# A 16-key band on attention weights: an added mask in TensorE's accumulation, or a product on VectorE behind the sigmoid

## The reference, cut to what matters

```python
idx = t - 1 - w                       # w = 0..15
valid = idx >= 0
nb = where(valid, z[:, clip(idx)], 0) # keys and values of the window
tau = sigmoid(einsum('bthd,bthwd->bthw', q, nb_k) / sqrt(8))
msg = einsum('bthw,bthwd->bthd', tau, nb_v)
y = x + msg.reshape(B, T, D) @ wo.T   # then a layer norm over D, gamma, beta
```

## Time and profile before

| | |
|---|---|
| median of 3 runs | 229.62 us (228.37 to 230.73) |
| the profiled execution | 228.22 us |
| its span in the trace | 226.5 us |
| span by the granted TensorE clock, mean | 0.856 |
| second attention, first scores to last value matmuls | 81.41 to about 128 us of the span |

### The profile page before, as it was taken

How to read it: one execution, slowest core, us unless ns; L and a number is a source line. 1 busy time by engine, 2 the same in 40 slices (tenths; PEclk the granted TensorE clock), 3 DMA queues, 4 the chain that set the end, 5 groups by cost and what they waited for, 6 DMA issues and landing times.

```text
span 226.5 us, 4763 instructions
## 1 busy us (share of the span) xinstructions
PE 176.7 (78%) x1677; PEld 132.3 (58%) x1677; DVE 115.2 (51%) x353; ACT 115.0 (51%) x268; POOL 63.3 (28%) x93
## 2 busy tenths in 40 slices
PE   2769689999997969995999959999720009999990
PEld 1327467776654534653568537999620008999980
DVE  6466685479855420530161479796475003555530
ACT  3756633886778555861463816422490003556540
POOL 8998002005200040000020020000674720355442
PEclk9979955799999788996799988999955555999996
DMA  4456355290003510250000399000000338000000
GB/s 118 123 129 191 73 177 153 53 335 6 9 1 85 174 35 0 87 170 26 3 0 3 103 367 269 4 3 0 3 0 23 117 114 283 26 16 26 26 10 0
DMA packets 21085, 18.91 MB, mean 84 GB/s; under 512 B 4029, under 2 KB 18608, under 8 KB 21062
## 3 DMA queue, kind: packets, MB, share of 16 engines
q1 hardware_dynamic: 19606, 16.86, 24.9%
q0 software_dynamic: 896, 1.59, 2.1%
q10 hardware_dynamic: 560, 0.16, 0.3%
HBM read 8.54 MB, written 4.03 MB: 55 GB/s over the span
## 4 chain that ended last, share of the span: by engine, by line
PE 59%; DVE 12%; DMA 8%; SPq 7%; issue 5%; POOL 4%; ACT 4%; DVEq 0%; POOLq 0%
PE ps L1018 7%; SPq L394 6%; PE ps L1031 6%; PE ps L891 6%; PE ps L611 5%; PE ps L848 5%; DMA t_Ks<-t_parts 4%; PE ps L828 4%; PE ps L677 4%; PE ps L814 3%; PE ps L606 3%; POOL z_dram L589 3%; DVE t_mx L1413 3%; PE ps L817 3%; PE ps L714 2%
## 5 line engine op out<-in xcount | busy, mean ns | idle before, releaser
L1325 ACT ACTIVATE t_v_pad<-ps,t_b_tile 128x128 f32<-128x128 f32 x60 | 17.2, 368 | 32.2 <-PE ps L1018 32.2
L1168 ACT ACTIVATE t_P<-ps 128x512 f32<-128x512 f32 x32 | 19.1, 603 | 18.4 <-PE ps L817 18.2
L1413 DVE TENSOR_REDUCE t_mx<-ps 128x4 f32<-128x512 f32 x32 | 21.8, 688 | 10.8 <-PE ps L677 10.3
L1136 ACT ACTIVATE t_P<-ps 128x512 f32<-128x512 f32 x32 | 18.8, 601 | 8.3 <-PE ps L700 3.9
L559 POOL TENSOR_SCALAR t_rstd<-t_mv 128x4 f32<-128x4 f32 (+2 forms) x5 | 1.4, 279 | 75.0 <-DVE t_mv L1482 75.0
L594 POOL DMA_INDIRECT out_dram<-t_v_pad,t_Qs x15 | 15.1, 1006 | 25.1 <-DVE t_v_pad L1684 24.4
L1018 PE MATMUL ps<-t_zsT,t_late 128*128 128x128 f32 x120 | 17.8, 297 | 0.2 <-DVE t_zsT L1680 0.2
L1010 PE MATMUL ps<-t_ident,t_Qs 128*128 128x128 f32 x15 | 4.3, 304 | 16.9 <-DMA t_Qs<-z_dram 16.9
L814 PE MATMUL ps<-t_bandb,t_identb 128*128 128x512 bf16 x32 | 13.5, 421 | 4.9 <-DMA t_Ks<-t_parts 4.9
L1542 DVE SCALAR_TENSOR_TENSOR t_Qs<-t_v_pad,t_mod,t_blend 128x128 f32<-128x128 f32 x64 | 17.1, 347 | 0.1
L1031 PE MATMUL ps<-t_Ks,t_v_pad 128*128 x120 | 16.9, 284 | 0.0
(11 more groups left out here) (265 smaller groups left out, 361.9 us busy)
## 6 DMA issues: line engine op xcount, KB each, us to landing
t_Qs<-t_parts SPq DMA_DIRECT2D x24, 128.0 KB
t_Ks<-t_parts SPq DMA_DIRECT2D x24, 128.0 KB
t_Ks<-in_L_ffn_W_dram SPq DMA_DIRECT2D x1, 2048.0 KB, 9.5
z_dram<-t_empty_row SPq DMA_DIRECT2D x1, 1935.0 KB, 8.5
t_Qs<-z_dram SPq DMA_DIRECT2D x1, 1032.0 KB, 6.9
t_Qs<-z_dram SPq DMA_DIRECT2D x1, 645.0 KB, 4.2
t_rows<-in_fside_BxSxS_dram SPq DMA_DIRECT2D x2, 256.0 KB, 3.2
t_x_tok<-in_x_dram SPq DMA_DIRECT2D x2, 256.0 KB, 3.7
```

The lines of the kernel that those rows point to most:

```text
L1136: act.activation(P[:, u % 3, :], SCORE_BANKS[u % 2][:, :], ACT.Exp, scale=SCALE).then_inc(scores_read, 1)
L1168: act.activation(P[:, (UNITS + u) % 3, :], ps[u % 4][:, :], ACT.Sigmoid, scale=SCALE).then_inc(window_scores_read, 1)
L1325: m = act.activation(hsT[:, n % 2, cs], ps[n % 2][:, cs], ACT.Gelu, bias=b1_tile[:, n % 2, c:c + 1])
L1413: dve.tensor_reduce(mx[:, b, 4 * g:4 * g + 4], MAX_BANKS[u % 2][:, :].rearrange("p (j t) -> p j t", j=4), AX.X, ALU.max).then_inc(max_scor ...
```

## The change

The band is no longer added to the scores. PE's matmul with `bandb` is gone, and each of the four score matmuls starts its own part of the bank. ACT takes the sigmoid of all 128x128 pairs. Then DVE multiplies the four heads' weights in place by `band`, a 32-bit matrix of ones and zeros (`keep_band`, one instruction of 128x512 a unit, placed last but for the residual in the unit's turn). PE's value matmuls wait for DVE's product in place of ACT's sigmoid. Since a unit's weights are alive for longer, `P` has four buffers instead of three, and the value matmuls and the output of a batch come one turn later (`LAG_WVALUES` 3, `LAG_WOUT` 6). `FRONT_AT` is computed from `LAG_WOUT` and moves by a turn too. The first attention uses the four buffers as well.

```diff
@@ -48,7 +48,7 @@
 
         ident = sb("ident", [128, 128])
         identb = sb("identb", [128, 128], BF16)
-        bandb = sb("bandb", [128, 128], BF16)
+        band = sb("band", [128, 128])
         onesb = sb("onesb", [128, 128], BF16)
         ones_row = sb("ones_row", [1, NT], BF16)
         mask_rows = sb("mask_rows", [NB, T], BF16)
@@ -90,7 +90,8 @@
         negmT = sb("negmT", [H, NB, T], BF16)
         sshift = sb("sshift", [128, NB, H])
         w_self = sb("w_self", [128, NB, H])
-        P = sb("P", [128, 3, 512])
+        RING = 4
+        P = sb("P", [128, RING, 512])
         pv_sb = sb("pv_sb", [128, 2, 256])
         den = sb("den", [128, 2, H])
         rden = sb("rden", [128, 2, H])
@@ -218,7 +219,7 @@
         HANDOFF = [half * HALF * G + HALF * G - 1 + LAG_OUT for half in range(2)]
 
         WINDOW_AT = UNITS + LAG_VALUES
-        LAG_WVALUES, LAG_WOUT = 2, 5
+        LAG_WVALUES, LAG_WOUT = 3, 6
         TURNS = WINDOW_AT + UNITS + LAG_WOUT
 
         FRONT_AT = WINDOW_AT + HALF * G - 1 + LAG_WOUT + 6
@@ -503,11 +505,11 @@
             pool.iota(empty_row[:, TOKEN:TOKEN + 1].bitcast(I32), pattern=[[0, 1]], base=NT, channel_multiplier=1)\
                 .then_inc(tile_zero, 1)
 
-            link(pool.memset(bandb[:], 0.0))
-            link(pool.affine_select(bandb[:], bandb[:], pattern=[[1, 128]], compare_op=ALU.is_ge,
-                                    fill=MASKED, base=-1, channel_multiplier=-1))
-            pool.affine_select(bandb[:], bandb[:], pattern=[[-1, 128]], compare_op=ALU.is_ge,
-                               fill=MASKED, base=WINDOW, channel_multiplier=1).then_inc(band_ready, 1)
+            link(pool.memset(band[:], 1.0))
+            link(pool.affine_select(band[:], band[:], pattern=[[1, 128]], compare_op=ALU.is_ge,
+                                    fill=0.0, base=-1, channel_multiplier=-1))
+            pool.affine_select(band[:], band[:], pattern=[[-1, 128]], compare_op=ALU.is_ge,
+                               fill=0.0, base=WINDOW, channel_multiplier=1).then_inc(band_ready, 1)
             pool.wait_ge(ld_braw, 16)
             pool.tensor_copy(b_parts[:, 0, :], b_raw[:]).then_inc(b_split, 1)
             pool.wait_ge(b_split, 1)
@@ -712,7 +714,7 @@
                         pe.wait_ge(pv_read, b - 1)
                 for j in range(4):
                     m = pe.matmul(VALUE_BANKS[b % 2][32 * j:32 * j + 32, g // 2 * T:(g // 2 + 1) * T],
-                                  v_pad[:, b, pair_head(g, j), :], P[:, u % 3, j * T:(j + 1) * T],
+                                  v_pad[:, b, pair_head(g, j), :], P[:, u % RING, j * T:(j + 1) * T],
                                   start=(g % 2 == 0), stop=(g % 2 == 1))
                 m.then_inc(pv_done, 1)
 
@@ -805,28 +807,26 @@
                 if u == 0:
                     pe.wait_ge(max_scores_read, G * NB)
                     pe.wait_ge(scores_read, G * NB)
-                    pe.wait_ge(band_ready, 1)
                 if b % HALF == 0 and g == 0:
                     pe.wait_ge(stack_in[half_of(b)], 16 * (4 * NSLOT + 2))
                 if u >= 4:
                     pe.wait_ge(window_scores_read, u - 3)
                 bank = ps[u % 4]
-                pe.matmul(bank[:, :], identb[:], bc_mid(bandb[:], 4), start=True, stop=False)
                 for j in range(4):
                     h = quad_head(g, j)
-                    m = pe.matmul(bank[:, j * T:(j + 1) * T], stacked(Ks, b, h), stacked(Qs, b, h), start=False,
-                                  stop=(j == 3))
+                    m = pe.matmul(bank[:, j * T:(j + 1) * T], stacked(Ks, b, h), stacked(Qs, b, h), start=True,
+                                  stop=True)
                 m.then_inc(window_scores_full, 1)
 
             def window_values(b, g):
                 u = b * G + g
-                pe.wait_ge(window_scores_read, u + 1)
+                pe.wait_ge(banded, u + 1)
                 if g == 0:
                     job_wait_read(pe, f"bv_{half_of(b)}")
                     pe.wait_ge(pv_read, NB + b - 1)
                 for j in range(4):
                     m = pe.matmul(VALUE_BANKS[b % 2][32 * j:32 * j + 32, 0:T], v_pad[:, b, quad_head(g, j), :],
-                                  P[:, (UNITS + u) % 3, j * T:(j + 1) * T], start=(g == 0), stop=(g == G - 1))
+                                  P[:, (UNITS + u) % RING, j * T:(j + 1) * T], start=(g == 0), stop=(g == G - 1))
                 m.then_inc(pv_done, 1)
 
             def window_out(b):
@@ -1131,9 +1131,9 @@
                 if u == 0:
                     job_wait_read(act, "ks_0")
                     job_wait_read(act, "ks_1")
-                if u >= 3:
-                    act.wait_ge(pv_done, u - 2)
-                act.activation(P[:, u % 3, :], SCORE_BANKS[u % 2][:, :], ACT.Exp, scale=SCALE).then_inc(scores_read, 1)
+                if u >= RING:
+                    act.wait_ge(pv_done, u - RING + 1)
+                act.activation(P[:, u % RING, :], SCORE_BANKS[u % 2][:, :], ACT.Exp, scale=SCALE).then_inc(scores_read, 1)
 
             def shift_row(b):
 
@@ -1164,8 +1164,8 @@
 
             def window_weights(u):
                 act.wait_ge(window_scores_full, u + 1)
-                act.wait_ge(pv_done, UNITS + u - 2)
-                act.activation(P[:, (UNITS + u) % 3, :], ps[u % 4][:, :], ACT.Sigmoid, scale=SCALE).then_inc(window_scores_read, 1)
+                act.wait_ge(pv_done, UNITS + u - RING + 1)
+                act.activation(P[:, (UNITS + u) % RING, :], ps[u % 4][:, :], ACT.Sigmoid, scale=SCALE).then_inc(window_scores_read, 1)
 
             def window_pv(b):
                 act.wait_ge(pv_done, G * (NB + b + 1))
@@ -1464,6 +1464,14 @@
                     dve.wait_ge(ld_c, 16 * 11)
                     dve.tensor_scalar(wr_g[:], wr[:], gb2[:, 0:1], None, ALU.mult).then_inc(wrg_ready, 1)
 
+            def keep_band(u):
+
+                if u == 0:
+                    dve.wait_ge(band_ready, 1)
+                dve.wait_ge(window_scores_read, u + 1)
+                weights = P[:, (UNITS + u) % RING, :].rearrange("p (j t) -> p j t", j=4)
+                dve.tensor_tensor(weights, weights, bc_mid(band[:], 4), ALU.mult).then_inc(banded, 1)
+
             def window_v(half):
                 name = f"bv_{half}"
                 job_wait_full(dve, name)
@@ -1575,6 +1583,9 @@
                     u = t - LAG_PVTR - step
                     if 0 <= u < UNITS and u % G == G - 1:
                         normalise(u // G, step)
+                u = t - WINDOW_AT
+                if 0 <= u < UNITS:
+                    keep_band(u)
                 if t == WINDOW_AT + LAG_WVALUES + UNITS:
 
                     dve.wait_ge(pv_done, G * 2 * NB)
```

More of the change, by code:

```diff
@@ L325, in fused_layer @@
         band_ready = sem("band_ready")
+        banded = sem("banded")
         ema_ready, tau_ready, diff_ready, ema_exp = sem("ema_ready"), sem("tau_ready"), sem("diff_ready"), sem("ema_exp")
```

## The result

The changed kernel takes 234.83 us (median of 4 runs, 233.83 to 237.10) against 229.0 (4 runs, 227.31 to 230.73) for the kernel before on the same chip: 1.039, interval 1.0281 to 1.05. It is slower by 5.8 us. A ratio is taken over those runs of each kernel that lie within 1.5% of its fastest, so it can differ from the ratio of the medians. The profiled execution took 234.75 us, with a span of 233.0 (before 228.22 and 226.5).

The account below looks back on a forecast made before the run. PE was taken to bound the second attention's second half, with DVE becoming the bound after the change. The copy 3.7 us later, plus 1.5 and less 0.7 for the clock, gave 4.5 on 229.62: 234.1 us, range 230.3 to 237.0.

Parts of the forecast that it names:

- PE's turn without the band: PE's work for one unit of the second attention after the change: 0.67 us, or 1.15 at the half clock.
- The product: DVE's added 128x512 multiplication in each of 32 units: 0.69 us, and 0.73 from its start to the next.
- From unit 16 to the product of unit 18: Start of the second half, PE at the half clock: 4.7 us, from 103.58 to 108.3.
- POOL's wait and the norm: add_norm(0) in DVE's queue, from the end of the statistics to the end of the norm: 4.18 us.
- The last weights: End of the second half: ACT's weights of unit 31 stand behind the gate's sigmoid and end at 129.65.
- Unit 16 starts 0.75 us earlier: First half: PE reaches attn sooner, so projections and unit 16 start 0.75 us earlier, the latter at 103.58.
- One hole of 4 to 5 us beside add_norm(0): PE's value matmuls wait for products queued behind add_norm(0) on DVE; PE stands idle for some 4.6 us.
- The clock: Half clock behind PE's new idle time costs 1.5 us; a shorter first half-clock stretch ahead gives back 0.7.
- PE stays at the half clock: Rival: gaps in each turn keep PE at half clock through the whole second half; 237.1 us, chance 0.08.
- the saving comes through: Rival: PE's 4.7 us and the 0.75 us ahead of unit 16 arrive in full; 224.2 us, chance 0.06.
- the prediction's price of 0.23 for a unit: PE's time for one band matmul at the full clock, saved in each unit: 0.23 us, or 0.43 at half clock.

Follow-up runs that it names:

- b1: The changed kernel with ten dead matmuls of zeros ahead of each of the two waits for the stacks; 235.93 us, 1.0414.
- a2: The kernel before with its band matmul left out and nothing in its place, so no mask is applied; 232.7 us against 230.03.
- a1: The changed kernel with one 512-column matmul of zeros ahead of each unit's scores, DVE still applying the band; 237.61 us, 1.0283.
- c4: The changed kernel with the 512-column matmul of zeros in units 16 to 21 only; 239.13 us, 1.0605.
- a4: The kernel before with ten dead band matmuls ahead of each of the two waits for the stacks; 224.9 us, 0.9804.
- c3: a4 without its band matmul in the units, so no mask is applied; 223.24 us, 0.985.
- b3: The changed kernel with each DVE product cut from 128x512 to 128x4, order and lags kept; 236.84 us, 1.0429.
- a3: The kernel before with four buffers and the later value matmuls and outputs, band still added by PE; 230.69 us against 230.03.
- b2: The changed kernel with add_norm(0) cut in three pieces behind the products of units 24, 25 and 26; 239.38 us, 1.0519.
- c1: The changed kernel with the edits of b1 and b2 together; 235.33 us, 1.0348.
- c2: c1 with gate_sums moved ahead of the product of unit 30 in DVE's program; 231.03 us, 1.0247.

## Why the prediction was right in sign and short in size

The time, 234.83, lies 0.7 from the forecast and in the range, and that closeness is partly luck: the forecast was put on a median of 229.62, which with the fourth run is 229.0, and this takes 0.6 off a miss of 1.3. The difference is 5.8 us and not 4.5; by the stages of the profiled executions it is 6.9. By the steps of the prediction:

- **Right.** PE's turn without the band is 1.13 us at the half clock (103.75 to 104.88), forecast 1.15. The product is 0.689 us. From unit 16 to the product of unit 18 it was 4.6 us, forecast 4.7. POOL's wait and the norm took 4.17 us, forecast 4.18. The last weights do stand behind the gate's sigmoid.
- **"Unit 16 starts 0.75 us earlier" did not come.** From the first scores to unit 16 it is 23.24 us, before 22.92. The gain was there at first: PE took `attn` 4.03 us behind the first scores (84.54), before 5.36 (86.77). But at 0.50 from 84.0 to 89.6 us it needed 4.44 us from there to the projections, before 3.00, and reached them 8.47 us behind the first scores, before 8.36. That term leaned on a clock that it had not costed.
- **"One hole of 4 to 5 us beside add_norm(0)" was 1.5 us.** PE at half speed had less slack to wait away. Where the clock was held the hole was 3.8 (b1), so the step is right for a fast PE.
- **The clock is the step that failed.** The prediction put in 1.5 us behind the hole and took off 0.7 for a shorter first stretch, 0.8 net, and let PE leave the half clock behind unit 16 "as before". It stayed there for 20 us. With the clock terms left out, against the forecast's own steps, the trace is 1.07 us late at unit 16 (23.24 for 22.17), 1.45 to the end of the norm (15.72 for 14.27) and 0.68 from there to the copy (14.93 for 14.25): 3.2 where 0.8 stood. That the first two are the clock's is seen where it is held behind unit 16 (11.86 for 15.72 in b1) and in PE's 4.44 us to the projections; for the last 0.68 it isn't shown. The term had the wrong trigger. I read the half clock as something that an idle time starts and that ends by itself. It can start so: every idle time of PE of 2.5 us or more from 78 to 150 us in these traces had it. It also started without one (b1, behind idle times of at most 1.40 us). And among the units of this stage it is the band matmul that ended it. Without it the clock stays down with DVE's products (after) and without (a2), and with 512 columns of zeros in each unit it comes back (a1, c4); in a2 it came back at 123.3 us, beside `x1T_0`, which is other work. The Trainium skill (TensorE: Matmul & The Clock Gate, HAM oscillation — how this bites in real kernels) says that a wait for a transfer throttles PE, and the waits of 2.53 us before and 2.90 us after agree. The Trainium skill (TensorE: Matmul & The Clock Gate, What's actually happening) has a busy PE regain the full clock; 15.51 us of 15.51 busy at 0.50 in a2 speak against reading "busy" as the profile's busy time.
- **The rival "PE stays at the half clock"** had 0.08 and was nearest to the trace, for another reason than the one it gave. It blamed gaps in each turn; behind unit 16 a2 has none, and after is busy for 15.00 of 15.72 us. PE got the full clock back at 123.96, behind `x1T_0`, so its whole price wasn't paid. What was held against this rival was misread: from 50 to 55 us PE was busy for 4.81 of 5.00 us and waited once, 0.19 us and for ACT, so it says nothing of turns with gaps. b1 does: there the clock fell where PE waited only 1.40, 0.47 and 0.68 us at a time.
- **The rival "the saving comes through"** has a true core. Once the clock is held and nobody multiplies, the stage gets shorter: the band's removal is worth 1.56 us ahead of unit 16 and 2.60 behind it (a4 to c3); the prediction's price of 0.23 for a unit would give 3.7 for the second.

How the 6.9 us divide can be given only along one path, from single profiles: band out, +2.35 (a2), that is 4.2 saved (a4 to c3) and some 6.5 lost to the clock; the product's wait, its place in the order and the later values, +4.05 (b3), of which the four buffers and later values may be up to 1.6 (a3, inconclusive); its width, +0.5 (after). By another path the parts differ, since clock and hole stand in for each other: lifting either alone took at most 1.5 us from the stage (b1; a1 and b2 did not shorten it). Lifting both was tried in c1 and not reached, since the hole came back in another place; c1 took 0.9. Of the 5.2 that c2 took from the changed kernel's stage, 2.1 lie behind gate_0 (6.43 to 4.35), where `gate_sums` was moved. Open stay: what in the 512-column matmul raises the clock; what the product's width costs at a held clock; and what is left of the loss once the hole beside the norm is really gone.

## What to carry to other kernels

A matmul that "only" occupies PE may be what brings the clock back behind a wait, so before taking it out, fill the wait: ten dead matmuls ahead of each of two waits made the kernel before 2% faster (224.9 us), and then the removal shortened the stage by 4.2 us, which without the fills it had not. Work moved into an in-order engine's queue costs what stands ahead of it there (a norm with its wait for POOL) and what it holds up behind it (the gate's sums: 6.43 us from gate_0 to the copy, 4.35 with them moved); its own width cost 0.5 us in the changed kernel as it ran. And after a repair, look whether the trace has lost what was to be repaired: c1 was to have neither hole nor half clock, had both, and so tells nothing of the two together.

## What was not expected of the hardware

PE busy for 15.51 of 15.51 us with scores of 96 rows and values of 32 columns was granted 0.50 all the time, and the same units held 1.00 for 18.97 us when they began there (c3). The clock also fell where PE's idle times were 1.40, 0.47 and 0.68 us (b1). One 128x512 matmul of zeros a unit raised the clock in 5.8 us (c4). Removing 32 matmuls from the kernel before, with nothing in their place, gave no shorter time (232.7 against 230.03).
